# Causal attention rebuilt: row scores for the maxima, column scores on 64-row halves, and the weighing of each four heads in one piece one step later

## What is computed

```python
b, t, c = x.shape                      # 8, 512, 128
q = concatenate([q_c, rope(q_e)])      # 16 heads, 8 channels, from x by two matrices in a row
k = concatenate([k_c, rope(k_e)])
scores = einsum('bhqd,bhkd->bhqk', q, k) / sqrt(8)
scores = where(causal, scores, -inf)
att = softmax(scores, axis=-1)
y = einsum('bhqk,bhkd->bhqd', att, v)
out = y @ Wc
```

## Time and profile before

| what | value |
|---|---|
| median of 3 runs | 4156.12 us (4153.95 to 4156.75) |
| the profiled execution's own time | 4155.47 us |
| its span | 4153.7 us |
| TensorE busy | 92% of the span |
| DVE, ACT, POOL busy | 78%, 75%, 60% |
| mean granted TensorE clock | 0.971 |

### The profile page before, as it was taken

One profiled execution on the slowest core, in us unless ns is written; L12 is line 12 of the kernel. 1 busy time (PEld: TensorE's weight loads), 2 busy tenths in 40 slices (PEclk: granted clock), 3 DMA queues, 4 the chain that ended last, 5 costly groups with the idle time before them and its releaser, 6 DMA issues.

```text
span 4153.7 us, 101302 instructions
## 1 busy us (share of the span) xinstructions
PE 3814.5 (92%) x30950; PEld 2939.8 (71%) x31328; DVE 3258.6 (78%) x5635; ACT 3109.2 (75%) x7150; POOL 2498.3 (60%) x2247
## 2 busy tenths in 40 slices
PE   6999998899998999988999989999889999899998
PEld 4666665677766777766777667777667776677776
DVE  5877876888867888768888678887688886788876
ACT  4777776788866888857888668887578886688875
POOL 1221221777745777737777457776377774577763
PEclk9999999999998999998999989999989999999999
DMA  2111111000010000010000100000100000000002
GB/s 79 42 32 31 29 39 35 2 0 0 0 28 1 1 0 0 1 28 1 0 0 0 28 1 1 0 0 1 28 1 0 0 0 28 1 1 0 0 1 68
DMA packets 53261, 52.86 MB, mean 13 GB/s; under 512 B 13574, under 2 KB 40452, under 8 KB 51972
## 3 DMA queue, kind: packets, MB, share of 16 engines
q1 hardware_dynamic: 52996, 49.77, 4.5%
HBM read 28.77 MB, written 4.19 MB: 8 GB/s over the span
## 4 chain that ended last, share of the span: by engine, by line
issue 26%; PE 24%; ACT 24%; DVE 21%; ACTq 2%; DVEq 2%; POOL 1%; SPq 0%; DMA 0%; POOLq 0%
PE bank L357 19%; ACT sb_area L668 12%; DVE sb_ssq L1105 10%; DVE sb_smax L1116 6%; ACT sb_area L777 5%; PE bank L416 3%; ACT sb_lnb L786 3%; ACT sb_lnb L789 3%; DVE sb_area L1093 1%; PE bank L503 1%; POOL sb_area L1336 1%; DVE sb_nmx L1013 1%; DVE sb_area L1119 0%; PE bank L532 0%; DVE sb_area L1009 0%
## 5 line engine op out<-in xcount | busy, mean ns | idle before, releaser
L668 ACT ACTIVATE sb_area<-bank 128x512 f32<-128x512 f32 (+4 forms) x3029 | 1570.3, 553 | 259.0 <-PE bank L357 182.3
L357 PE MATMUL bank<-sb_area 128*64 128x64 f32 (+4 forms) x16624 | 1286.1, 274 | 94.9 <-issue 57.8
L1093 DVE TENSOR_TENSOR sb_area<-bank,sb_rots 128x1024 f32<-128x1024 f32 x768 | 939.2, 1224 | 395.2 <-ACT sb_area L777 394.4
L1311 POOL TENSOR_TENSOR sb_area<-sb_area,sb_rn 128x512 f32<-128x512 f32 x768 | 784.8, 1043 | 608.5 <-ACT sb_rn L793 608.5
L1297 POOL TENSOR_TENSOR sb_area<-sb_area 128x512 f32<-128x512 f32 x768 | 967.9, 1278 | 78.3 <-DVE sb_area L1093 76.2
L357 PEld LDWEIGHTS bank<-sb_area 128*64 128x64 f32 (+2 forms) x16624 | 849.5, 151 | 200.6 <-issue 139.1
L357 PE MATMUL bank<-sb_wqk_hi,sb_xwin 128*128 128x512 f32 x1536 | 729.7, 477 | 53.9 <-DVE sb_xwin L1073 43.6
L357 PE MATMUL bank<-sb_area,sb_wvo 128*128 128x256 f32 x3072 | 728.3, 381 | 3.1 <-DVE sb_xT L1151 3.1
L357 PEld LDWEIGHTS bank<-sb_area,sb_wvo 128*128 128x128 f32 x3072 | 555.0, 190 | 78.3 <-issue 12.8
L503 PE MATMUL bank<-sb_ident,sb_area 128*128 128x128 f32 x3072 | 494.9, 285 | 33.4 <-ACT sb_area L668 31.0
L503 PEld LDWEIGHTS bank<-sb_ident,sb_area 128*128 128x128 f32 x3072 | 358.8, 144 | 227.6 <-issue 160.0
(11 more groups left out here) (103 smaller groups left out, 4861.7 us busy)
## 6 DMA issues: line engine op xcount, KB each, us to landing
sb_xwin<-sb_p SPq DMA_DIRECT2D x256, 64.0 KB, 2.0
sb_area<-in_Wqkv SPq DMA_DIRECT2D x7, 1024.0 KB, 5.8
sb_area<-in_WvT SPq DMA_DIRECT2D x7, 512.0 KB, 7.3
sb_wo_bd<-in_Wo SPq DMA_DIRECT2D x14, 256.0 KB, 8.2
sb_area<-in_x SPq DMA_DIRECT2D x4, 512.0 KB, 5.7
sb_area<-in_x SPq DMA_DIRECT2D x8, 256.0 KB, 2.9
x_plus_causal<-sb_area SPq DMA_DIRECT2D x8, 256.0 KB, 2.3
out<-sb_area SPq DMA_DIRECT2D x8, 256.0 KB, 3.5
```

Of the source, the lines that this page charges most:

```text
L357: return nc.tensor.matmul(o, a, b, start=start, stop=stop, skip_group_check=True)
L668: return nc.scalar.activation(o, i, ACT.Copy)
L1093: tt_(t12[:, c % 2, :, :].rearrange("p u (h d) -> p u h d", h=8), src, bc(rots[:, tt, s, :, :], [P, 2, 8, D], 2), ALU.mult).then_inc(S["ro ...
L1311: pt_(qn[:, c, :].rearrange("p (h d) -> p h d", h=8), qsum[:, c % 2, :].rearrange("p (h d) -> p h d", h=8), r, ALU.mult).then_inc(S["qn"], 1)
```

## The change

The stage becomes 32 slots of 4 heads each (8 batches, 4 head groups), and all engines run steps -7 to 37, written out without a loop. In step s the engines work on three slots:

- **Row scores of slot s** (`rows_of_scores`, 8 units: 2 heads in parallel by 4 query tiles). They serve only for the maxima. The stacks now hold, for each channel of a head, four rows next to each other (three of the terms, without lo·lo, and one row for the maxima); two masks instead of four separate the heads, and one product uses 64 rows of the array: two heads run on the lower and the upper half, into banks 0 and 1. Four bf16 products of 64 rows add the mask. One DVE operation takes both heads' maxima from the two banks (`maxima`). Each unit waits for the maximum of the unit ahead, and each maximum for its unit.
- The maxima of slot s-1 are transposed on PE, split by ACT and DVE into two parts, stored to DRAM and loaded into two rows of each head's query operand, so that the product itself subtracts them.
- **Column scores of slot s-2** (`columns_of_scores`, 6 pairs): keys on partitions, queries on columns, again two heads on two halves, into banks 2 to 5. ACT takes exp, without bias and without sums, in 12 operations (`exp_pair`). No transposes and no copies of them are left.
- **Weighing of slot s-3** (`weigh_causal`), in one piece between unit 0 and pair 1: 16 fp32 products with 32 output rows each, four at a time side by side in the array. The values have columns of ones, so the sums come out too.

Queries, keys, values, the sums' move to the heads' rows (`move_sums`), the output product and the maxima share bank 7 in an order given by `m_at`. `xT` is read directly, without the copy L970. The inverse sum is Ln and Exp on ACT, and one DVE product of 128x512 a half batch divides. The output product is now 8 products of 128 columns a batch. The stacks are made by 6 DMAs to DRAM a batch and 2 loads of 256 KB a slot. POOL's zeroing of `v16` (L1264, 8704 columns) becomes one of 4096 columns. SP issues the first layer's weights after its step 37, so after the last batch's sum and its store.

The diff's core (the matching functions of before are removed; they are printed above):

```diff
         at[0] = 0
-        v16 = take(TT, HEADS * (P + DA))
-        ptA = take(4, TT, T)
-        ea_ = take(2, (TT + 1) * TT // 2 * P)
+        et0, et1, et2 = take(4, T), take(4, T - P), take(4, T - P)
+        v32 = take(2, TT * 4 * 2, 2, 32)
...
+        stack_q = wqk_hi[:, :].rearrange("p (g t) -> p g t", g=4)
+        stack_k = wqk_lo[:, :].rearrange("p (g t) -> p g t", g=4)
+        mrows = ptT[:, :, 0:2, :]
...
+            def split_out(a):
+                sp.wait_ge(S["c_split"], 4 * a + 4)
+                for term in range(3):
+                    sp.dma_start(qk_rows[a % 2, 0, :, term, :], split_qk[:, 0, term // 2, :].bitcast(F32)).then_inc(S["qk_out"], 16)
+                    sp.dma_start(qk_rows[a % 2, 1, :, term, :], split_qk[:, 1, term % 2, :].bitcast(F32)).then_inc(S["qk_out"], 16)
+            def stack(n, side, stk, name):
+                a, hg = n // 4, n % 4
+                sp.wait_ge(S["rows_out0"], 2 * 16)
+                sp.wait_ge(S["rows_out1"], 2 * 16)
+                sp.wait_ge(S["qk_out"], 6 * 16 * (a + 1))
+                sp.dma_start(stk[:, hg, :].bitcast(F32),
+                             qk_rows[a % 2, side, 32 * hg:32 * hg + 32, :, :].rearrange("h e t -> (h e) t")).then_inc(S[f"{name}{hg}"], 16)
+            def max_rows(n):
+                sp.wait_ge(S["m_free"], m_at["max", n] + 1)
+                sp.dma_start(mx_rows[n % 2].rearrange("e q t -> q e t"), mrows[0:16, n % 2, :, :].bitcast(F32)).then_inc(S["mx_out"], 16)
+                sp.wait_ge(S["mx_out"], 16 * (n + 1))
+                for part in range(2):
+                    sp.dma_start(qm[3 + 4 * part:P:64, n % 4, :, :].rearrange("p x t -> p (x t)").bitcast(F32),
+                                 mx_rows[n % 2, part].rearrange("(g q) t -> g (q t)", g=2)).then_inc(S[f"mrow{n % 4}"], 16)
+            for s in range(FIRST, LAST + 1):
+                if slot(s - 1):
+                    max_rows(s - 1)
+                if slot(s + 1):
+                    need(sp, "c_s2", 12 * (s - 2))
+                    stack(s + 1, 1, stack_k, "stack_k")
+                if s % 4 == 0 and valid(s // 4 + 1):
+                    split_out(s // 4 + 1)
+                if slot(s + 2):
+                    need(sp, "qm_ready", 2 * (s - 1))
+                    stack(s + 2, 0, stack_q, "stack_q")
+                if s % 4 == 1 and valid((s - 9) // 4):
+                    a = (s - 9) // 4
+                    sp.wait_ge(S["m_free"], m_at["out", a] + 1)
+                    sp.dma_start(scr[a], xres[:, 1, :, :]).then_inc(S["ca_out"], 16)
+                    if valid(a + 1):
...
                     break
-                if l == 0:
-                    sp.wait_ge(S["ca_sum"], B)
...
             def project_causal(a, i):
...
-                    m.then_inc(S["v_mm"], 1)
...
+            def turn_max(n):
+                o = bank_m("max", n)
+                pe.wait_ge(S["c_max"], 8 * n + 8)
+                nc.tensor.transpose(o[0:32, 0:P], nmx[:, n % 2, :], ident[:, :]).then_inc(S["c_mt"], 1)
+            def move_sums(a, j):
+                o = bank_m("perm", a, j)
+                pe.wait_ge(S["c_yraw"], 2 * a + j + 1)
+                mm(o, perm, yraw).then_inc(S["c_perm"], 1)
+            def causal_out(a):
+                o = bank_m("out", a)
+                pe.wait_ge(S["yT_ready"], 2 * a + 2)
+                for t in range(TT):
+                    mm(o[:, t * P:(t + 1) * P], yT[:, 0, t * P:(t + 1) * P], wc[:, 0, :], True, False)
+                    m = mm(o[:, t * P:(t + 1) * P], yT[:, 1, t * P:(t + 1) * P], wc[:, 1, :], False, True)
+                m.then_inc(S["ca_mm"], 1)
+            def rows_of_scores(n, u):
+                hg, x, qt = n % 4, u // 4, u % 4
+                need(pe, "c_max", 8 * n + u)
+                if u == 0:
+                    pe.wait_ge(S["qm_ready"], 2 * n + 2)
+                    pe.wait_ge(S[f"stack_k{hg}"], 16 * (n // 4 + 1))
+                keys, queries = (qt + 1) * P, slice(qt * P, (qt + 1) * P)
+                low, high = slice(0, 64), slice(64, P)
+                for g, rows in ((0, low), (1, high)):
+                    mm(ps[g][:, 0:keys], qm[rows, n % 4, x, queries], stack_k[rows, hg, 0:keys], True, False)
+                for g, rows in ((0, low), (1, high)):
+                    mm(ps[g][:, queries], identb[rows, :], tri[rows, :], False, False)
+                for g, rows in ((0, low), (1, high)):
+                    mm(ps[g][:, queries], identb2[rows, :], tri2[rows, :], False, True).then_inc(S["c_s1"], 1)
+            def columns_of_scores(n, p):
+                hg, T_, x = n % 4, p // 2, p % 2
+                need(pe, "c_exp", 12 * n + 2 * p - 2)
+                if p == 0:
+                    pe.wait_ge(S[f"mrow{hg}"], 2 * 16 * (n // 4 + 1))
+                b0 = ps[2 + 2 * p % 4], ps[3 + 2 * p % 4]
+                low, high = slice(0, 64), slice(64, P)
+                blocks = (((0, 0),), ((1, 0),), ((2, 0), (3, 2 * P)))[T_]
+                for kt, c0 in blocks:
+                    for g, rows in ((0, low), (1, high)):
+                        mm(b0[g][:, c0:c0 + T - kt * P], stack_k[rows, hg, kt * P:(kt + 1) * P], qm[rows, n % 4, x, kt * P:T], c0 == 0, False)
+                for kt, c0 in blocks:
+                    for g, rows in ((0, low), (1, high)):
+                        mm(b0[g][:, c0:c0 + P], tri[rows, :], identb[rows, :], False, False)
+                    for g, rows in ((0, low), (1, high)):
+                        m = mm(b0[g][:, c0:c0 + P], tri2[rows, :], identb2[rows, :], False, True)
+                        if kt == blocks[-1][0]:
+                            m.then_inc(S["c_s2"], 1)
+            def weigh_causal(n, kt):
+                a, hg = n // 4, n % 4
+                pe.wait_ge(S["c_exp"], 12 * n + (4, 8, 12, 12)[kt])
+                if kt == 0 and hg % 2 == 0:
+                    pe.wait_ge(S["m_free"], m_at["v", a] + 1)
+                    need(pe, "c_yraw", 2 * a + hg // 2)
+                e, c0 = ((et0, 0), (et1, 0), (et2, 0), (et2, 2 * P))[kt]
+                for r in range(4):
+                    m = mm(ps[6][32 * r:32 * r + 32, kt * P:T], v32[:, a % 2, (kt * 4 + r) * 2 + hg // 2, hg % 2, :],
+                           e[:, r, c0:c0 + T - kt * P], hg % 2 == 0 and kt == 0, hg % 2 == 1 and kt == 3)
+                    if kt != 2:
                         m.then_inc(S["c_pv"], 1)
-                if (n == 17 and part) or n == SLOTS + 17:
-                    after = b if n < SLOTS else b + 1
-                    pe.wait_ge(S["yT_ready"], after)
-                    for t in range(TT):
-                        m = mm(ps[7][:, t * P:(t + 1) * P], yT[:, t * P:(t + 1) * P], wc)
...
+                pair(0)
+                if slot(n1 - 1):
+                    turn_max(n1 - 1)
+                unit(0)
+                for kt in range(TT):
+                    weigh(n2 - 1, kt)
+                pair(1)
+                unit(1)
+                if k == 0 and valid(s // 4):
+                    causal_values(s // 4)
+                if k == 1 and valid((s - 9) // 4):
+                    causal_out((s - 9) // 4)
+                if k == 2 and valid((s + 6) // 4):
+                    project_causal((s + 6) // 4, 1)
+                if k == 3 and valid((s + 5) // 4):
+                    project_causal((s + 5) // 4, 2)
+                pair(2)
+                unit(2)
+                unit(3)
+                pair(3)
+                if k == 0 and valid((s - 4) // 4):
+                    move_sums((s - 4) // 4, 0)
+                if k == 1 and valid((s + 7) // 4):
+                    project_causal((s + 7) // 4, 0)
+                if k == 2 and valid((s - 6) // 4):
+                    move_sums((s - 6) // 4, 1)
+                if k == 3 and valid((s + 5) // 4):
+                    project_causal((s + 5) // 4, 3)
+                unit(4)
+                pair(4)
+                unit(5)
+                pair(5)
+                unit(6)
+                unit(7)
...
+            def exp_pair(n, p):
+                if not slot(n):
+                    return
+                T_, x = p // 2, p % 2
+                w = T if T_ == 0 else T - P
+                need(act, "c_pv", 12 * (n - 1) + 4 * T_ + 4)
+                for g in range(2):
+                    act.wait_ge(S["c_s2"], 12 * n + 2 * p + g + 1)
+                    nc.scalar.activation((et0, et1, et2)[T_][:, 2 * g + x, :], ps[2 + (2 * p + g) % 4][:, 0:w], ACT.Exp)                        .then_inc(S["c_exp"], 1)
+            def heads_of_max(n):
+                act.wait_ge(S["c_mt"], n + 1)
+                if n >= 2:
+                    act.wait_ge(S["mx_out"], 16 * (n - 1))
+                copy(mrows[0:32, n % 2, 0, :], ps[7][0:32, 0:P]).then_inc(S["c_mh"], 1)
+            def weighed_causal(a, j):
+                act.wait_ge(S["c_pv"], 12 * (4 * a + 2 * j + 2))
+                need(act, "yT_ready", 2 * a + j)
```

(93 more changed lines are left out.)

294 lines of the change are left out of this document (110 added, 184 removed).

## The result

| | before | after |
|---|---|---|
| median of the runs compared (4 each), us | 4156.43 | 4092.7 (4091.25 to 4095.09) |
| ratio, 95% interval | | 0.9848 [0.9831, 0.9865] |
| profiled execution: own time, span, us | 4155.5, 4153.7 | 4091.25, 4089.3 |
| first unit's scores; first layer's weights issued, us | 60.75; 709.9 | 60.54; 641.98 |

The account below looks back on a forecast made before the run. A chain of units, maxima and weighing, lengthened by half clock, was taken to bound the new causal stage: 58 + 32 x 17.3 + 15 + 7.2 = 633.8 instead of 709.9, so -76 from 4155.5: 4079 us, range 3990 to 4175.

Parts of the forecast that it names:

- The step: Causal stage, one step of 4 heads: 15.7 us at full clock, 17.3 with half clock, instead of 20.3.
- The clock's share: Half clock in some steps, from the thin part into the next weighing: 3.5 us each, 1.6 a step on average.
- The two units in front: First two units of a step at half clock: 0.8 us lost together.
- The other engines: Causal stage: DVE 9.1 and ACT 7.6 us a step; no engine fills the step, a chain bounds it.
- The clock holds: Rival for the causal stage: full clock throughout, 15.7 us a step, kernel 4028 us; chance 0.25.
- Four columns don't share: Rival: the weighing's four columns don't share the array, 8.5 instead of 2.5 us, step 23.3, kernel 4271; chance 0.07.
- Changes of tiling cost 0.2 each: Rival: five changes of tiling a step cost 0.2 us each, 32 us in all, kernel 4111; chance 0.12.
- Half clock throughout: Rival for the causal stage: half clock in every step, 23.2 us a step plus cold ends, kernel 4270; chance 0.08.
- The start: Before the causal stage's first unit: first unit at 58 us instead of 60.75.
- The end: After the last unit: column scores of two slots, a weighing and the DRAM way, 15 us.
- The tail: Last batch's output product, sum and store before the first layer's weights are issued: 7.2 us newly on the path.

Follow-up runs that it names:

- the filler kernel: Seven fp32 products of 128 columns with zeros added per step behind units 6 and 7, against the kernel after: 4044.99 us, step 15.76.
- the half weighing: Half of the weighing's products of three key tiles left out (6 of 16), against the kernel after: 4091.57 us, step 17.17.
- the loads-first kernel: SP issues the first layer's weights ahead of the last batch's sum and store, against the kernel after: 4085.73 us, ratio to before 0.983.

## Why the prediction was right, and what of the 12 us it missed

**The step.** Sum 553.6 us for 32 steps (32 x 17.3), measured 612.88 - 60.54 = 552.3, from the first unit to the last transpose. The terms: units with handover 0.53, 0.58, 0.64, 0.70 at full clock (forecast 0.62 to 0.79); one at half clock 0.4 more, as forecast (1.10 here, from 603.04 to 604.14, against 0.70 from 364.95 to 365.65); from the maximum 3 of one step to its maximum 7, 360.92 to 366.88, 5.96 us, and 6.2 on average where the clock was full (forecast 2.63 + 3.29 + 0.4 = 6.3); the weighing at most 2.5 with its two masks (forecast 2.5 without them), 4.0 where mostly at half clock.

**The clock's share.** It was put at 1.6 us a step and is 17.23 - 15.76 = 1.5 by the filler kernel. The size is right, but partly by luck: 1.6 was chosen and not summed. The prediction expected half clock in some steps, at 3.5 us each. The trace shows it in every one of the 31 steps, at about 1.5 us each (16.4 to 17.6 us against 15.0 to 15.9). The two units in front, priced at 0.8 together, kept the full clock in 18 of the 31 steps; what was slowed is the weighing, 4.03 us instead of 2.51. Twice as many steps at less than half the price give the same sum.

**The other engines.** Their work was covered, as forecast, but for DVE's conversions beside POOL (last section): over the steady part the only waits of PE that its view lists (total us, times, longest) are for the maxima.

The rows of the unit at half clock, then the waits of PE:

```profile
603.04 0.79 PE L387 MATMUL bank<-sb_wqk_lo,sb_xwin 64*128 64x512 f32 x2 [1.08 <-DVE sb_area L1130]
604.14 1.23 DVE L1130 TENSOR_REDUCE sb_area<-bank 128x2 f32<-128x1024 f32 x1 [1.16 <-PE bank L387]
```
```profile
PE bank L387 <- DVE sb_area L1130: 68.2, 74, 1.8
PE bank L432 <- DVE sb_area L1130: 21.2, 23, 1.0
```

**The rivals.** *The clock holds* had its step right (15.7 a step; 15.76 in the filler kernel) and its condition wrong. Gaps of about 1.2 us did not keep the clock up: PE was busy 1.6 of 3 us in the thin part, and the clock fell behind it. The filler kernel is close to this rival made true: 4045, where the rival said 4028 with a start and an end that were themselves 8 us too good. *Four columns don't share* fell with the half weighing. *Changes of tiling cost 0.2 each* would put the filler kernel's step at 16.7 rather than 15.76. The Trainium skill (TensorEngine Tiling (Array Packing), Tiling Modes) says that such a change drains TensorE; by that rule a price was to be expected, and the step of the filler kernel leaves none beyond the terms counted. No run changes the tilings alone, so a small price, set off by a term that was put too high, isn't ruled out. *Half clock throughout* would show 0.5; the steady part shows 0.85.

**The start**, forecast 58, was 60.54. The prediction gave its "more DMA than before" no number of its own inside the 58. The rows of queries and keys land in 4.0 us here, where the store of the earlier trace rows took 2.3; six of them are issued one behind the other, so 4.0 isn't the price of one alone. That is 1.7 us by reading the trace; the other 0.8 has no place.

**The end** was the largest miss. "Column scores of two slots remain, each 6.2 us of ACT, with a weighing and the DRAM way: 15 us" measured 633.1 - 612.88 = 20.2. ACT idles inside it:

```profile
613.19 3.97 PE L387 MATMUL bank<-sb_area 128*32 128x512 f32 x32
615.27 1.09 ACT L822 ACTIVATE sb_area<-bank 128x512 f32<-128x512 f32 x2 [5.84 <-PE bank L387]
...
622.67 2.51 PE L387 MATMUL bank<-sb_area 64*128 64x128 bf16 x34
```

The exps of one slot wait for a weighing to free their buffer, and the next slot's wait for the next weighing. With the last one, three weighings lie in this stretch, where the sum had one: from 613.19 on, mostly at half clock, from 622.67 and from 630.45.

**The tail** of 7.2 us was 641.98 - 633.1 = 8.9: the output product took 3.58 us, mostly at half clock (0.58 in 637 to 641), for its 8 products (16 instructions) instead of 2 (above, 637.11). The loads behind it take 10.5 us to the first copy, 641.98 to 652.51, where they took 9.5. A store of the batch's sum stands just ahead of them on the queue, but it explains at most half: in the loads-first kernel, without that store ahead, they still take 10.0, 635.53 to 645.57. That the tail was on the path at all is what the loads-first kernel shows.

**The account:** start +2.5, steps -1.3, end +5.2, tail +1.7, loads +1.0: 9.1 us of the 12. The profiled execution lies 1.5 below its median. The layers behind, unchanged in code, took 3436.8 us from the first copy to the span's end against 3434.3, and 2.5 us are not explained; the later kernels show 3437.3 to 3438.9 there. Start, end and layers were read in the traces and not changed by themselves, so their causes are argued, not shown; only the tail was moved by an experiment, and that shows that it was on the path, not why it was long.
